# A four-layer graph network on one core: a new order of work, an early flag, and the layer-two mask moved from TensorE to GpSimd

## What is computed

```python
def layer0(x, adj, W, a):            # graph attention
    Wh = x @ W.T
    e = leaky_relu((Wh @ a1)[:, None] + (Wh @ a2)[None, :], 0.2)
    return softmax(where(adj == 0, -inf, e)) @ Wh
def layer1(x, adj, ...):             # "layer two" of the title
    h = x @ W
    e = leaky_relu((h @ a_1).T + h @ a_2 + h @ a_12 @ h.T, 0.2)
    att = softmax(where(adj > 0, e, -9e15))
    return elu(x @ W_1 + (att @ x) @ W_2)
def layer2(x, adj, ...):             # four heads
    s = where(adj | eye, q @ k.T / sqrt(32), lowest)
    return relu((softmax(s) @ v) @ Wo + bo)
def layer3(x, adj, ...):             # relations; adj holds 0 and 1 here
    return relu((adj.T == 1) @ ((h + b) * sigmoid(g + bg)))
for layer in (layer0, layer1, layer2, layer3):
    x = layernorm(x + layer(x, adj))
```

## Time and profile before

| what | value |
| --- | --- |
| time, median of 3 runs | 518.59 us (518.09 to 518.69) |
| the profiled execution's own time | 518.74 us |
| its span, first to last instruction | 516.9 us |
| PE busy | 478.7 us (93%) |
| ACT busy | 425.1 us (82%) |
| DVE busy | 397.7 us (77%) |
| POOL busy | 317.7 us (61%) |
| mean granted clock of PE | 0.984 |

### The profile page before, as it was taken

The page is one execution under the profiler, slowest core; times in us unless marked ns, Lnnn a source line. Parts: engine busy times, 40 slices in busy tenths (PEclk is TensorE's granted clock), DMA queues, the critical chain, the costliest instruction groups (busy, mean ns, idle before and its releaser), DMA issues. The chain is left out here.

```text
span 516.9 us, 14050 instructions
## 1 busy us (share of the span) xinstructions
PE 478.7 (93%) x3964; PEld 411.4 (80%) x3964; DVE 397.7 (77%) x1558; ACT 425.1 (82%) x1261; POOL 317.7 (61%) x717
## 2 busy tenths in 40 slices
PE   3767899999999999999999999999999999999880
PEld 2556788888888898888888888888888888888660
DVE  3486788889888888889888888888987888766540
ACT  2444999989988888999898888898998988898740
POOL 3054456566766766666666676766676676664562
PEclk9988999999999999999999999999999999999996
DMA  6121101122122211222122221122212200000111
GB/s 188 30 83 41 42 13 53 53 63 61 55 63 62 62 44 37 58 63 63 52 64 62 63 58 31 49 63 62 63 52 64 62 23 22 22 22 22 32 32 30
DMA packets 40220, 26.92 MB, mean 52 GB/s; under 512 B 2641, under 2 KB 39889, under 8 KB 40146
## 3 DMA queue, kind: packets, MB, share of 16 engines
q1 hardware_dynamic: 40146, 26.03, 17.4%
HBM read 17.63 MB, written 8.39 MB: 50 GB/s over the span
## 5 line engine op out<-in xcount | busy, mean ns | idle before, releaser
L744 ACT ACTIVATE p<-p,nmax 128x256 f32<-128x256 f32 x256 | 126.6, 498 | 0.4 <-DVE nmax L941 0.4
L1140 POOL TENSOR_SCALAR x<-y,minus_mean,rstd 128x128 f32<-128x128 f32 x256 | 114.7, 458 | 17.7 <-issue 15.9
L1122 POOL TENSOR_TENSOR rstd<-ve,minus_half 128x2 f32<-128x2 f32 x128 | 101.9, 796 | 0.0
L941 DVE CUSTOM_DVE_ANT_0 p<-ps,neg 128x256 f32<-128x256 f32 x256 | 92.7, 419 | 6.6 <-PE ps L520 6.6
L1115 POOL TENSOR_SCALAR ve<-stats 128x2 f32<-128x2 f32 x128 | 24.7, 193 | 110.8 <-DVE stats L854 105.6
L753 ACT COPY p2T<-ps 128x512 f32<-128x512 f32 x128 | 75.0, 595 | 0.0
L531 PE MATMUL ps<-ident,p 128*128 128x128 f32 x512 | 71.7, 273 | 1.5 <-ACT p L744 1.5
L531 PEld LDWEIGHTS ps<-ident,p 128*128 128x128 f32 x512 | 57.4, 141 | 3.2 <-DVE nmax L941 1.4
L977 DVE SCALAR_TENSOR_TENSOR y<-ps,x 128x256 f32<-128x256 f32 x32 | 13.7, 427 | 56.6 <-PE ps L576 56.6
L854 DVE BATCH_NORM_STATS2 stats<-y 128x6 f32<-128x256 f32 x128 | 53.2, 415 | 2.3
L662 ACT COPY xT<-ps 128x256 f32<-128x256 f32 x96 | 36.6, 382 | 17.6 <-PE ps L400 17.1
(11 more groups left out here) (134 smaller groups left out, 1232.3 us busy)
## 6 DMA issues: line engine op xcount, KB each, us to landing
adj_in<-in_adj_dram SPq DMA_DIRECT2D x32, 256.0 KB, 3.0
xT<-in_xT_dram SPq DMA_DIRECT2D x32, 128.0 KB, 2.8
x_in<-in_x_dram SPq DMA_DIRECT2D x32, 128.0 KB, 3.0
x_aside<-x SPq DMA_DIRECT2D x32, 128.0 KB, 2.2
out_dram<-x SPq DMA_DIRECT2D x32, 128.0 KB, 1.8
l_w<-in_l_w_dram SPq DMA_DIRECT2D x1, 257.0 KB
l_w<-in_l_w_dram SPq DMA_DIRECT2D x1, 256.0 KB
first_w<-in_first_w_dram SPq DMA_DIRECT2D x1, 129.0 KB, 2.2
```

The lines of the kernel that those rows point to most:

```text
L744: last = nc.scalar.activation(p2(n)[:, k, a, :], p2(n)[:, k, a, :], ACT.Exp, bias=nmax2(n)[:, k, a:a + 1], scale=-1.0, accum_out=sum2(n)[: ...
L941: last = nc.vector.tensor_tensor_reduce(p2(n)[:, k, a, :], bank("sc2", n, a)[:, k * N:(k + 1) * N], neg2(n)[:, k, :], -1.0, HIGHEST, ALU.a ...
L1122: nc.gpsimd.tensor_tensor(rstd[layer](n), ve[layer](n), minus_half[:, :], ALU.pow)\
L1140: last = nc.gpsimd.tensor_scalar(dst[:, k, 0:D], y_t[layer](n)[:, k, :], minus_mean[layer](n)[:, k:k + 1], rstd[layer](n)[:, k:k + 1], ALU ...
```

## The change

- **Flag.** DVE compares its maximum with 1, PE sums over partitions with one small product, DVE makes the flag: steps flag_a, flag, flag_b. The all-reduce on POOL goes.
- **Unit matrix.** DVE writes 0 to 127 into each row by doubling, PE turns one row into a column of a bank, DVE compares the two. `lift` and `not_eye` are made from it.
- **Weights.** `setup_later` becomes four steps, prep_a to prep_d, with places of their own, and so do their ACT copies.
- **Output bias.** wo2 loses the product L556; y2 becomes y2a (adds bo from a full-precision row) and y2b (relu and residual).
- **Mask of layer one.** z1 loses L483. POOL adds neg1 to the relu'd scores in a new step, rmask1, and e1 waits for that; neg1 is a step of its own on DVE.
- **Last norms.** For the last three graphs DVE applies the norms of layers two and three.
- **Loads.** One step becomes four; adj has 5 buffers instead of 3, eq1 7 instead of 8.
- **Order.** Every place in PLAN is new.

```diff
-    "tensor": [("proj0", 1186), ("s2_rows", 1340), ("pT0", 2529), ("agg0", 2749), ("xT1", 3690), ("tT", 3889),
+    "tensor": [("proj0", 10866), ("s2_rows", 11031), ("pT0", 11536), ("prep_a", 11687), ("agg0", 11743),
...
-    "wo2": [("b", "y2_ready")],
+    "wo2": [("b", "y2a_ready")],
...
             def setup():
+                pe.wait_ge(sem("index_step"), 5)
+                pe.matmul(ps[:, 3, 0:P], index[0:1, :], ones_row[:, :], start=True, stop=True)\
+                    .then_inc(sem("setup_pe"), 1)
...
+            def flag(n):
+                o = bank("flag", n)
+                bank_free(pe, "flag", n)
+                pe.wait_ge(sem("excess_ready"), 2)
+                pe.matmul(o[0:1, 0:1], excess[:, :], xw0_all[:, 0, 0, D + 2:D + 3], start=True, stop=True)\
+                    .then_inc(sem("excess_ps"), 1)
...
             def z1(n):
                 o = bank("z1", n)
                 bank_free(pe, "z1", n)
-                pe.wait_ge(sem("masks_ready"), n + 1)
-                pe.matmul(o, ident_bf[:, :], neg1(n).rearrange("p t n -> p (t n)"), start=True, stop=False)
                 pe.wait_ge(sem("tT_sb"), n + 1)
...
             def wo2(n):
...
-                    pe.matmul(o[:, k * D:(k + 1) * D], onT(n)[:, k * P:(k + 1) * P], l2_w[:, WO],
-                              start=True, stop=False)
-                    last = pe.matmul(o[:, k * D:(k + 1) * D], ones_bf[:, :], bo_parts[:, :],
-                                     start=False, stop=True)
+                    last = pe.matmul(o[:, k * D:(k + 1) * D], onT(n)[:, k * P:(k + 1) * P], l2_w[:, WO],
+                                     start=True, stop=True)
...
             def e1(n):
-                dve.wait_ge(sem("relu_ready"), n + 1)
+                dve.wait_ge(sem("rmask_ready"), n + 1)
...
+            def y2b(n):
+                dve.wait_ge(sem("y2a_ready"), n + 1)
+                nc.vector.scalar_tensor_tensor(out=y_t[2](n), in0=y_t[2](n), scalar=0.0, in1=x2(n)[:, :, 0:D],
+                                               op0=ALU.max, op1=ALU.add).then_inc(sem("y2_ready"), 1)
...
+            def rmask1(n):
+                pool.wait_ge(sem("neg1_ready"), n + 1)
+                pool.wait_ge(sem("relu_ready"), n + 1)
+                nc.gpsimd.tensor_tensor(relu(n), relu(n), neg1(n), ALU.add).then_inc(sem("rmask_ready"), 1)
```

More of the change, by code:

```diff
@@ L26 @@
 PLAN = {
[L27 removed]
[15 rows of a table removed]
+    "sync": [("ld_xT", 9192), ("ld_adj", 9857), ("ld_w", 10128), ("ld_x", 10629), ("aside", 17031), ("store", 18181)],
[6 rows of a table added]
+        ("c_prep_c", 12330), ("c_prep_d", 12406), ("c_xT1", 12408), ("c_tT", 12433), ("relu1", 12516),
[12 rows of a table added]
 }
 RING = {
[1 row of a table removed]
[1 row of a table added]
     "x1": 3, "xT1": 2, "tT": 2, "xw1": 3, "relu": 2, "p1": 2, "p1T": 2, "h": 2, "hexp": 2,
@@ L51 @@
 }
-FIRST_BANK = {"a": 0, "b": 4}
-WEIGHTS_AFTER = 0
+BANKS = {"a": (0, 1, 2, 3), "b": (4, 5, 6, 7)}
+AT_END = 3
+GRAPHS = {
+    **{step: (0, 1) for step in ("ld_w", "prep_a", "prep_b", "prep_c", "prep_d",
+                                 "c_prep_a", "c_prep_b", "c_prep_c", "c_prep_d")},
+    **{step: (-1, 0) for step in ("flag_a", "flag", "flag_b")},
+    **{step: (0, -AT_END) for step in ("norm2", "norm3")},
+    **{step: (-AT_END, 0) for step in ("end_norm2", "end_norm3")},
+}
 PSUM_USES = {
@@ L83, with graphs_of @@
     "agg3": [("b", "y3_ready")],
-}
+    "prep_a": [], "prep_b": [], "prep_c": [], "prep_d": [],
+    "flag": [("b", "flag_ready")],
+}
+def graphs_of(step, graphs):
+    first, end = GRAPHS.get(step, (0, 0))
+    return range(first if first >= 0 else graphs + first, end if end > 0 else graphs + end)
 def program(engine, graphs):
@@ L330, in _ @@
             sp.dma_start(first_w[:, :], t["first_w"]).then_inc(sem("w0_loaded"), 16)
-            run("sync", {"load": load, "aside": aside, "store": store})
+            run("sync", {"ld_adj": ld_adj, "ld_xT": ld_xT, "ld_x": ld_x, "ld_w": ld_w, "aside": aside, "store": store})
             for s in range(RING["x4"]):
@@ L443, in s2_rows @@
                 last.then_inc(sem("s2_ps"), 1)
-                if n == 0:
-                    setup_later()
             def rs_rows(n):
@@ L623, in _ @@
             run("tensor", {
+                "prep_a": prep_a, "prep_b": prep_b, "prep_c": prep_c, "prep_d": prep_d, "flag": flag,
                 "proj0": proj0, "s2_rows": s2_rows, "rs_rows": rs_rows, "pT0": pT0, "agg0": agg0, "xT1": xT1_, "tT": tT_, "xw1": xw1_, "z1": z1, "pT1": pT1,
@@ L806, in setup @@
             def setup():
-                nc.vector.memset(bias_rows[:, :], 0.0)
-                nc.vector.memset(last_row[:, :], 0.0).then_inc(sem("dve_setup"), 1)
-                nc.vector.memset(ax_row[:, :], 0.0)
-                nc.vector.memset(minus_half[:, :], -0.5)
-                nc.vector.memset(ones_bf[:, :], 1.0).then_inc(sem("dve_setup"), 1)
+                for k in range(8):
+                    last = nc.vector.memset(index[:, k:k + 1], float(k))
+                last.then_inc(sem("index_step"), 1)
+                nc.vector.memset(ones_row[:, :], 1.0)
+                for k, size in enumerate((8, 16, 32, 64)):
+                    dve.wait_ge(sem("index_step"), k + 1)
+                    last = nc.vector.tensor_scalar(index[:, size:2 * size], index[:, 0:size], float(size), None, ALU.add)
+                    last.then_inc(sem("index_step"), 1)
+                nc.vector.memset(lift[:, P - 1:P], 0.0)
                 nc.vector.memset(xw0_all[:, :, :, D + 2:D + 3], 1.0)
@@ new lines, in end_norm @@
+            def end_norm(layer, n):
+                dve.wait_ge(sem(f"mean{layer}_ready"), n + 1)
+                dve.wait_ge(sem(f"rstd{layer}_ready"), n + 1)
+                dst = (x3, x4)[layer - 2](n)
+                if layer == 2:
+                    free(dve, "x3", n, "y3_ready")
+                    if n >= RING["x3"]:
+                        dve.wait_ge(sem(f"x3_aside{n % RING['x3']}"), 16 * (n // RING["x3"]))
+                if layer == 3 and n >= RING["x4"]:
+                    dve.wait_ge(sem(f"stored{n % RING['x4']}"), 16 * (n // RING["x4"]))
+                if n == B - AT_END:
+                    dve.wait_ge(sem(f"x{layer + 1}_ready"), n)
+                for k in range(T):
+                    last = nc.vector.tensor_scalar(dst[:, k, 0:D], y_t[layer](n)[:, k, :],
+                                                   minus_mean[layer](n)[:, k:k + 1], rstd[layer](n)[:, k:k + 1],
+                                                   ALU.add, ALU.mult)
+                last.then_inc(sem(f"x{layer + 1}_ready"), 1)
@@ new lines, in flag_a, with flag_b @@
+            def flag_a(n):
+                dve.wait_ge(sem("eq1_ready"), B)
+                nc.vector.tensor_reduce(excess_max[:, :], excess_col[:, :], AX.X, ALU.max)\
+                    .then_inc(sem("excess_ready"), 1)
+                dve.wait_ge(sem("excess_ready"), 1)
+                nc.vector.tensor_scalar(excess[:, :], excess_max[:, :], 1.0, None, ALU.is_gt)\
+                    .then_inc(sem("excess_ready"), 1)
+            def flag_b(n):
+                dve.wait_ge(sem("excess_ps"), 1)
+                nc.vector.tensor_scalar(excess_flag[:, :], bank("flag", n)[0:1, 0:1], 0.5, None, ALU.is_gt)\
+                    .then_inc(sem("flag_ready"), 1)
```

177 lines of the change are left out of this document (83 added, 94 removed), and 33 rows, old and new, of tables (PLAN, RING).

## The result

The changed kernel takes **546.85 us** (median of 4 runs, 545.03 to 547.98) against 518.64 for the kernel before on the same chip: a ratio of 1.0542, 95% interval 1.0506 to 1.0578. It is slower by 28 us. The prediction said 522 in a range of 499 to 538. The sign came out (it gave 0.47 to slower, so that is little more than a toss), but the size lies outside the range. The profiled execution took 545.84 us, with a span of 543.9.

The account below looks back on a forecast made before the run. PE bound the old kernel at 14.43 us a round; a queue loop of 14.86 was to replace it. 39.3 + 40.2 + 371.5 + 43.1 + 26.6, plus 1.8 outside the span, made 522.5; forecast 522, range 499 to 538.

Parts of the forecast that it names:

- Start, -11 us: Until sc2 of graph 0: earlier unit matrix and exp0 were to bring it to 39.3 instead of 50.24 us.
- End, -5 us: From sc2 of graph 31 to the end: 26.6 instead of 31.6 us, mostly by dropping POOL's all-reduce.
- What leaves PE: Per round, L483's slot of 0.21 and the output bias's 0.16 go; PE's sum falls 0.37 to 14.06 us.
- The loop: Queue order closes a chain xT2 to xT2 over PE, ACT, DVE, POOL: 14.74 us, with the clash 14.86 per round.
- my three stretches: Loop parts: PE, xT2 to xw1's end, 8.04; ACT, to exp2a's end, 2.95; c_elu1 over y1b and norm to xT2, 3.75.
- the clash: DVE's neg1 delays POOL's power of var1 in layer two; it was to add 0.12 us per round.
- The second loop: c_xw1, c_xT3, exp2a, c_elu1, c_xT1, exp0, then pT0 and round to xw1: about 14.5 us.
- The first and last rounds: First three rounds 40.2 us (before 38.5), last three 43.1 (before 35.8), each shortened for steps missing there.
- Clash strikes rmask1: Third rival: DVE's eq1 or neg1 delays rmask1, or it costs 1.8; rounds 15.1 to 15.5, 539 us; chance 0.18.
- by my own sign: If rs_rows waits for e1, or rmask1 lasts over 1.3 us, the third rival holds.
- e1's path has no slack: y1b over norm, rmask1 and e1 to rs_rows takes 5.3 us, as does the way by xT2, agg0 and qk2.
- PE stays the bound: Rival: the loop is misjudged by 0.7 us, rounds take PE's 14.06, total 493.5 us; chance 0.22.

## Why the prediction was wrong in size

**Start, -11 us: right in sum, its cause only half.** exp0 of graph 0 begins at 9.04 (9.5 predicted) and sc2 at 36.69. But with the same edits in the old order exp0 begins at 9.29 and sc2 of graph 0 at 44.48: 5.8 of the 13.6 us come from the edits, 7.8 from the new order, in which a graph passes from proj0 to agg3 in 6.1 rounds of the table, where the old one took 8.5.

**End, -5 us: nearly right.** 4.0, and 5.0 in the old order with the mask on PE (26.6).

**What leaves PE: right.** The round of 14.26 in the old order with the mask on PE confirms 0.16 for the bias; the slot of the mask's product there is 0.22 (0.21). The rest, 14.04, is PE's work; the new order has the same products, but no run of it is free of waits.

**The loop is there, and the mis-sized step is its third stretch.** Of my three stretches, the first measured 8.13 (8.04), the second 2.93 (2.95), the third 4.39 (3.75, and 0.12 for the clash). 0.09 - 0.02 + 0.64 - 0.12 = 0.59, the whole of 15.45 less 14.86, and 0.52 of it is the third stretch. The failed sentence is "I add 0.12": minus_mean, power and norm were each held, by neg1, y2b and eq1, for 0.14, 0.14 and 0.24, which is 0.52 where I had 0.12, and the hand-overs took the other 0.12 of the 0.64. I had looked at one pair, and left out y2b's two SBUF operands and eq1 beside the norm. The run without these showed 15.10 us, 12 us less. Over 25 rounds and the few longer ones the 0.59 is 15.3 us, 13 of them from this stretch.

**The second loop, mis-sized too.** I put it at "about 14.5" without showing its terms; the changed kernel's rows give 14.90, and the runs without the power and without DVE's work have rounds of 14.90, 15.07 and 15.10 by it. So the round would have been at least 14.90, with a clash of any size: my 14.86 was out of reach, and a cut in the first loop's own part was worth 0.35 to 0.55 and not the 0.8 to 0.95 that I expected of the power.

**The first and last rounds.** I let the steps that are missing there shorten them (40.2 and 43.1; by my own terms the first is 12.97 + 2 x 13.97 = 40.9). They took 45.9 and 47.0, 9.6 more: about 15.3 and 15.7 a round, as long as a full one. That they are so long because layers two and three, on which the loop lies, run in them is argued and not tested. With 15.3, 2.6 less at the start and 0.95 more at the end this gives 23.2, the difference of the span from my 520.7.

**The rivals.** "Clash strikes rmask1" had rounds of 15.1 to 15.5 and 539 us, nearest to the result, but not its mechanism: rmask1 did take 1.33 (1.29 in the mean), so by my own sign this rival held, and yet taking the addition away left 547.0. My sentence that e1's path has no slack, with 0.1 in the round for each 0.1 of rmask1, doesn't hold here: rs_rows and proj0 behind e1 would be through at 267.89, and sc2 begins at 268.09, when c_qk2 is done. "PE stays the bound" is what the old order does: 501.

**What I didn't see at all.** First, that the loop has a branch of nearly its own length over DVE's queue to r1 (0.23 shorter, from the run with xw1 moved), and that PE's queue in the new order holds 0.9 us of smaller waits beside the one for norm1. They are read by taking the slots of PE, start to start, in the changed kernel and in the fastest one (the six that grew; they sum to 1.4):

| slot on PE (us) | old order, mask on PE | new order | who is waited for |
|---|---|---|---|
| s2_rows | 0.22 | 0.31 | |
| xw1 | 0.87 | 0.97 | |
| pT2b0 | 0.44 | 0.62 | agg1 for c_xw1 |
| tT | 0.43 | 0.74 | pT0 for exp0 |
| pT2b1 and pT2a1 | 0.87 | 1.42 | xT2 for norm1 |
| proj0 | 0.45 | 0.65 | sc2 for c_qk2 |

The wait of tT's slot is the second loop's. So a cut in the trunk won 0.38 to 0.55 a round and no more: with norm1 early, the second loop sets 14.9 to 15.1. Second, that POOL's mask, harmless in the new order, costs the old one 0.5 us a round as it was placed: 0.44 of PE's waits are for the bank of z1, 0.26 for that of s2_rows, and the mask's product of 0.22 is saved. The runs with the bank moved (14.59) and with e1 later (15.33, a wait of 0.92) change that wait and the round together; a placement that takes it away wholly wasn't found, and whether 14.04 could be reached so stays open.

## What to carry to other kernels

A table of places that brings a graph through in fewer rounds can win only once, at the start, and can cost in each round: here, with the mask on PE in both orders, the new one wins 4.8 us until sc2 of the first graph (38.28 for 43.12) and loses 48.5 between this and sc2 of the last. Before such a change, follow the chain from an engine back to itself through every queue, all branches of it, and compare its length with the busiest engine's work; if it is longer, no edit of work off the chain helps, however long an engine waits for it. A cut in the chain wins only down to the next one, so work out the second longest with the same care: here 14.90 behind 15.45. And try edits and order apart: the edits without the order and the mask gave 0.965, the bundle 1.054.

## What the runs showed of the hardware

DVE's mask (tensor_scalar, int32 to bf16, 128x512) took 0.41 to 0.42 alone and 1.39 and 1.37 beside a two-operand addition and a product of POOL that began 0.09 and 0.24 earlier (1.20 and 1.32): it ended 0.28 and 0.29 behind them, so it was held for nearly their whole length. Of POOL's short operations beside DVE's, minus_mean went from 0.23 to 0.37, the power from 0.71 to 0.85 or 1.06, a norm's two halves from 0.90 to 1.14 and, in other places, 1.40. The 1.06 is what eq1 still had to run (0.36 of it left, 0.35 longer); the others are less than that: 0.29 of neg1 and of y2b was left when minus_mean and the power began, and each took 0.14 longer; the norm's second half began 0.11 ahead of eq1 and still took 0.24 longer. Why they come out so short, no run shows. The Trainium skill ("SBUF — State Buffer", "SBUF: two separate sides") says that a DVE operation in a two-port mode, or with two SBUF inputs, and a GpSimd one exclude each other for an operation's whole length. The 1.39 and 1.37 agree with it, if the mask, which has one input, runs in such a mode, which no run here shows; a norm held by an operation that by the records began after it does not fit as it stands.
